# Query, key and value projections of the first linear attention from fp32r high and low parts, on a Trainium2 core

## The reference, cut to what matters

```python
for i in range(8):
    residual = x
    Q  = elu(x @ Wq[i] + bq[i]) + 1      # 16 heads of 64 = 1024 columns
    Kf = elu(x @ Wk[i] + bk[i]) + 1
    V  = x @ Wv[i] + bv[i]
    KV, sumK = sum_s(Kf * V), sum_s(Kf)  # over the 32 tokens of a batch entry
    att = Q * KV / (Q * sumK + 1e-06)
    y = gelu(att @ Wo[i] + bo[i])
    x = layer_norm(y + residual) * ln1_s[i] + ln1_b[i]
    residual = x
    h = gelu(gelu(x @ W1[i] + b1[i]) @ W2[i] + b2[i])
    x = layer_norm(h + residual) * ln2_s[i] + ln2_b[i]
```

## Time and profile before

| | us |
|---|---|
| median of 3 runs (lowest to highest) | 2660.99 (2655.34 to 2661.57) |
| the profiled execution's own time | 2657.94 |
| its span, first to last instruction | 2656.1 |
| attention, first projection (662.0) to last x (1956.3) | 1294.3 |

### The profile page before, as it was taken

The page is one execution under the profiler, slowest core; times in us unless marked ns, Lnnn a source line. Parts: engine busy times, 40 slices in busy tenths (PEclk is TensorE's granted clock), DMA queues, the critical chain, the costliest instruction groups (busy, mean ns, idle before and its releaser), DMA issues. The chain is left out here.

```text
span 2656.1 us, 29174 instructions
## 1 busy us (share of the span) xinstructions
PE 2419.6 (91%) x9257; PEld 1357.0 (51%) x9278; DVE 2144.5 (81%) x2857; ACT 1883.3 (71%) x2673; POOL 791.4 (30%) x466
## 2 busy tenths in 40 slices
PE   7899999998799999999999999999866899757998
PEld 3467776663344444444444444444323677444776
DVE  5787878872899999999999999999857888486454
ACT  6565555654789888998988898888756777435444
POOL 0121121111444444444444444444300000000554
PEclk9999999999899999999999999999986999977999
DMA  2000000002000101001010100100000011310211
GB/s 73 13 21 17 17 20 17 17 1 87 2 0 0 40 1 40 0 0 40 0 40 0 40 0 0 40 0 0 0 12 23 32 40 39 98 41 16 77 65 48
DMA packets 40927, 67.74 MB, mean 26 GB/s; under 512 B 15128, under 2 KB 31832, under 8 KB 39640
## 3 DMA queue, kind: packets, MB, share of 16 engines
q1 hardware_dynamic: 40512, 64.13, 7.4%
q10 hardware_dynamic: 288, 2.10, 0.2%
HBM read 60.91 MB, written 5.31 MB: 25 GB/s over the span
## 5 line engine op out<-in xcount | busy, mean ns | idle before, releaser
L251 PE MATMUL a_ps<-a_x,a_w 128*128 128x512 f32 x1536 | 695.4, 598 | 25.9 <-DVE a_kf L599 13.4
L251 PEld LDWEIGHTS a_ps<-a_x,a_w 128*128 128x128 f32 x1536 | 291.6, 191 | 405.1 <-issue 367.8
L774 POOL TENSOR_TENSOR a_den<-a_qf,a_ksum 128x1024 f32<-128x1024 f32 x128 | 271.0, 2117 | 512.0 <-DVE a_qf L592 475.3
L777 POOL TENSOR_TENSOR a_num<-a_qf,a_kvsum 128x1024 f32<-128x1024 f32 x128 | 294.8, 2303 | 185.5 <-DVE a_kvsum L617 185.5
L2705 ACT ACTIVATE x_sqk<-x_b_k 128x512 f32<-128x512 f32 x256 | 152.9, 597 | 149.1 <-PE x_b_k L2617 142.7
L2781 DVE TENSOR_REDUCE x_rn<-x_sqk 128x8 f32<-128x512 f32 x256 | 174.1, 681 | 91.7 <-ACT x_sqk L2705 87.4
L262 PE MATMUL a_ps<-a_att,a_w 128*128 128x512 f32 x480 | 215.8, 592 | 0.0
L592 DVE SCALAR_TENSOR_TENSOR a_qf<-a_eq,a_qf 128x1024 f32<-128x1024 f32 x128 | 195.2, 1525 | 1.7
L445 ACT ACTIVATE a_den<-a_den,consts 128x1024 f32<-128x1024 f32 x128 | 147.0, 1149 | 55.4 <-POOL a_den L774 55.4
L2598 POOL TENSOR_TENSOR x_kn<-x_craw,x_w 128x256 f32<-128x256 f32 x64 | 47.0, 734 | 464.5 <-DVE x_craw L2770 442.9
L599 DVE SCALAR_TENSOR_TENSOR a_kf<-a_ek,a_ps 128x1024 f32<-128x1024 f32 x128 | 155.4, 1214 | 29.6 <-ACT a_ps L441 24.7
(11 more groups left out here) (423 smaller groups left out, 5189.1 us busy)
## 6 DMA issues: line engine op xcount, KB each, us to landing
a_w<-layers SPq DMA_DIRECT2D x8, 2577.0 KB, 9.7
x_craw<-ctx SPq DMA_DIRECT2D x32, 256.0 KB, 2.7
y_cx<-ctx_t SPq DMA_DIRECT2D x16, 512.0 KB, 3.7
m_wb<-m_scratch SPq DMA_DIRECT2D x16, 512.0 KB, 3.8
n_w<-experts SPq DMA_DIRECT2D x8, 544.0 KB, 5.0
x_w<-xattn_w ACTq DMA_DIRECT2D x1, 1536.0 KB, 9.4
x_all<-x_t SPq DMA_DIRECT2D x4, 256.0 KB, 9.4
...
```

Source lines behind the costliest of these rows:

```text
L251: last = nc.tensor.matmul(bank(tile, j), col(par, part * HK + u * P, P), x[:, t0:t0 + BANK], start=True, stop=True)
L774: nc.gpsimd.tensor_tensor(by_batch(den[:, b, :]), by_batch(qf[:, b, :]), bcast(ksum[:, b, :], S), ALU.mult).then_inc(d_ready, 1)
L777: nc.gpsimd.tensor_tensor(by_batch(num[:, b, :]), by_batch(qf[:, b, :]), bcast(kvsum[:, b, :], S), ALU.mult).then_inc(n_ready, 1)
```

## The change

Every projection is made of three fp32r matmuls in place of one f32 matmul: high weight by high x, high weight by low x, low weight by high x. The high part is a copy into fp32r, the low part the difference. VectorE makes both parts of x at the end of each tail (high x, Hx, from z, and low x, Lx), and TensorE waits for Lx (`x_split`) at the start of a window, now ahead of `out(0)`. GpSimd splits the weights unit by unit (a copy and a subtraction of 128 x 384) in the odd windows 1 to 13, each behind that unit's last projection; SyncE loads each unit's raw weights as the split before ends. The weights of layer 0 are split at the start, and its x by ScalarE (high) and VectorE (low), in four parts. The two gelus of a tail write back into tile_t instead of g, which takes waits for g away; the gelus of W1 write into att, so hid is gone. ScalarE's q part waits for GpSimd behind its exponential and no longer ahead of it. The order is another on every engine; GpSimd's list is written out too.

The diff, without these lists and without what only follows from the rest:

```diff
+UCOLS = 3 * P
+RCOLS = WCOLS + BCOLS - CH * UCOLS
...
+        x_hi, x_lo = (sb(n, [P, TOK], F32R) for n in ("x_hi", "x_lo"))
+        w = sb("w", [P, 2, RCOLS])
+        w_raw = sb("w_raw", [P, UCOLS])
+        w_hi, w_lo = (sb(n, [P, CH, UCOLS], F32R) for n in ("w_hi", "w_lo"))
...
-        hid = sb("hid", [P, FCH, HALF])
-
+
+        first_raw = att[:, 1, 0:3, :].rearrange("p a b -> p (a b)")
...
+            sp.dma_start(first_raw, layers_dram[0][:, 0:CH * UCOLS]).then_inc(first_loaded, 16)
             for par in range(2):
-                sp.dma_start(w[:, par, :], layers_dram[par]).then_inc(w_loaded[par], 16)
+                sp.dma_start(w[:, par, :], layers_dram[par][:, CH * UCOLS:]).then_inc(w_loaded[par], 16)
...
+                for layer in range(LAYERS - 1):
+                    for u in range(CH):
+                        sp.wait_ge(w_split, 8 * layer + u + 8)
+                        sp.dma_start(w_raw[:, :], layers_dram[layer + 1][:, u * UCOLS:(u + 1) * UCOLS]).then_inc(raw_loaded, 16)
+                    if layer + 2 < LAYERS:
+                        wait_ahead(sp, affine, 4 * layer + 4)
+                        sp.wait_ge(x_high, 2 * layer + 2)
+                        sp.dma_start(w[:, layer % 2, :], layers_dram[layer + 2][:, CH * UCOLS:]).then_inc(w_loaded[layer % 2], 16)
...
+                def project(v, half, u, part):
+                    n = 8 * v + u
                     tile, free, ready = ((tile_q, q_parts, q_ready), (tile_k, k_feat, k_ready),
                                          (tile_v, kv_prod, v_ready))[part]
                     wait_past(pe, free, n)
+                    if not half:
+                        pe.wait_ge(w_split, 4 * v + (u + 1))
+                    c = slice(part * P, (part + 1) * P)
                     for j in range(2):
-                        t0 = half * HALF + j * BANK
-                        last = nc.tensor.matmul(bank(tile, j), col(par, part * HK + u * P, P),
-                                                x[:, t0:t0 + BANK], start=True, stop=True)
+                        t = slice(half * HALF + j * BANK, half * HALF + (j + 1) * BANK)
+                        for p, (a, b) in enumerate(((w_hi, x_hi), (w_hi, x_lo), (w_lo, x_hi))):
+                            last = nc.tensor.matmul(bank(tile, j), a[:, u, c], b[:, t], start=(p == 0), stop=(p == 2))
                     last.then_inc(ready, 1)
...
-                    out(0)
                     if not half:
                         pe.wait_ge(w_loaded[par], 4 * v - 8 * par + 16)
-                    wait_ahead(pe, affine, 2 * v - 2)
+                    pe.wait_ge(x_split, v + 1)
+                    out(0)
+                    out(2)
+                    k_of(0)
                     q_of(0)
-                    k_of(0)
-                    out(2)
                     v_of(0)
-                    q_of(1)
                     k_of(1)
                     out(4)
+                    q_of(1)
+                    k_of(2)
                     v_of(1)
-                    k_of(2)
                     out(6)
                     q_of(2)
                     v_of(2)
...
+                    wait_past(act, q_feat, n - 1)
+                    act.wait_ge(q_ready, n + 1)
+                    nc.scalar.activation(eq[:, b, :], tile_q[:, :], ACT.Exp, bias=bias(par, C_BQ + u)).then_inc(q_exp, 1)
+                    wait_past(act, d_ready, n - 1)
                     wait_past(act, n_ready, n - 1)
-                    act.wait_ge(q_ready, n + 1)
-                    nc.scalar.activation(eq[:, b, :], tile_q[:, :], ACT.Exp, bias=bias(par, C_BQ + u))
                     nc.scalar.activation(qf[:, b, :], tile_q[:, :], ACT.Relu, bias=bias(par, C_BQ + u)).then_inc(q_parts, 1)
...
-                    wait_ahead(act, normed, 2 * v)
                     wait_ahead(act, wo_done, v + 1)
-                    nc.scalar.activation(g[:, :], tile_t[:, :], ACT.Gelu_apprx_tanh, bias=bias(par, C_BO)).then_inc(gelu_done, 1)
+                    nc.scalar.activation(tile_t[:, :], tile_t[:, :], ACT.Gelu_apprx_tanh, bias=bias(par, C_BO)).then_inc(gelu_done, 1)
...
+                for p in range(4):
+                    c = slice(p * BANK, (p + 1) * BANK)
+                    nc.scalar.activation(x_hi[:, c], x[:, c], ACT.Copy).then_inc(first_high, 1)
...
+                def high_of(half, scale, shift):
+                    nc.vector.tensor_scalar(x_hi[:, half * HALF:(half + 1) * HALF], z[:, :], scale, shift,
+                                            ALU.mult, ALU.add).then_inc(x_high, 1)
...
+                    def high_x():
+                        if tail:
+                            wait_ahead(dve, normed, 2 * tv + 2)
+                            high_of(th, bias(tp, C_S2), bias(tp, C_B2))
+
+                    def low_x():
+                        if tail:
+                            t = slice(th * HALF, (th + 1) * HALF)
+                            dve.wait_ge(x_high, v)
+                            wait_ahead(dve, affine, 2 * tv + 2)
+                            nc.vector.tensor_tensor(x_lo[:, t], x[:, t], x_hi[:, t], ALU.subtract).then_inc(x_split, 1)
...
+                def numerator(n, b):
                     pool.wait_ge(kv_summed, n + 1)
+                    pool.wait_ge(q_feat, n + 1)
...
+                def split_unit(u, raw, done):
+                    nc.gpsimd.tensor_copy(w_hi[:, u, :], raw).then_inc(w_high, 1)
+                    pool.wait_ge(w_high, done + 1)
+                    nc.gpsimd.tensor_tensor(w_lo[:, u, :], raw, w_hi[:, u, :], ALU.subtract).then_inc(w_split, 1)
...
+                    def split(u):
+                        if half and more:
+                            for ready in (q_ready, k_ready, v_ready):
+                                pool.wait_ge(ready, 8 * v + (u + 1))
+                            pool.wait_ge(raw_loaded, 64 * v + (16 * u - 48))
+                            pool.sem_inc(w_begun, 1)
+                            split_unit(u, w_raw[:, :], 4 * v + (u + 4))
...
+                pool.wait_ge(first_loaded, 16)
+                for u in range(CH):
+                    split_unit(u, first_raw[:, u * UCOLS:(u + 1) * UCOLS], u)
+                all_windows(pool, window, tail_alone)
```

More of the change, by code:

```diff
@@ L231, in all_windows @@
             window(last + 1, 1, 0, True)
-            window(last + 2, 1, 1, True)
+            window(last + 2, 1, 1, True, False)
             tail_alone(last + 2, 1)
@@ L397, in down_part @@
                             pe.wait_ge(hid_gelu, 4 * v + 4 * j + c + 1)
-                            last = nc.tensor.matmul(bank(tile_t, j), col(par, C_W2 + c * D, D), bank(hid[:, c, :], j),
+                            last = nc.tensor.matmul(bank(tile_t, j), col(par, C_W2 + c * D, D), bank(hid(1, c), j),
                                                     start=(c == 0), stop=(c == FCH - 1))
@@ L629, in add_residual @@
                     wait_ahead(dve, affine, z_read)
-                    nc.vector.scalar_tensor_tensor(out=z[:, part], in0=g[:, part], scalar=1.0, in1=resid,
+                    nc.vector.scalar_tensor_tensor(out=z[:, part], in0=tile_t[:, part], scalar=1.0, in1=resid,
                                                    op0=ALU.mult, op1=ALU.add).then_inc(z_added, 1)
@@ L635, in centre, with normalise @@
                     nc.vector.tensor_tensor(z[:, part], z[:, part], tile_t[:, part], ALU.subtract).then_inc(z_centred, 1)
-                def normalise(k, out, scale, shift, part=slice(0, HALF)):
+                def normalise(k, part=slice(0, HALF)):
                     dve.wait_ge(rstd, k + 1)
@@ L640, in normalise, with scale_shift @@
                                                    op0=ALU.mult, op1=ALU.mult).then_inc(normed, 1)
+                def scale_shift(k, out, scale, shift, part=slice(0, HALF)):
                     wait_ahead(dve, normed, k + 1)
@@ L645, in x_of, with window @@
                     return x[:, half * HALF:(half + 1) * HALF]
-                def window(v, par, half, tail):
+                def high_of(half, scale, shift):
+                    nc.vector.tensor_scalar(x_hi[:, half * HALF:(half + 1) * HALF], z[:, :], scale, shift,
+                                            ALU.mult, ALU.add).then_inc(x_high, 1)
+                def window(v, par, half, tail, more=True):
                     tv, tp, th = v - 1, par if half else 1 - par, 1 - half
@@ L765, in _ @@
                     dve.sem_inc(sem_ahead, 1)
+                for p in range(4):
+                    c = slice(p * BANK, (p + 1) * BANK)
+                    dve.wait_ge(first_high, p + 1)
+                    ins = nc.vector.tensor_tensor(x_lo[:, c], x[:, c], x_hi[:, c], ALU.subtract)
+                    if p % 2:
+                        ins.then_inc(x_split, 1)
                 all_windows(dve, window, tail_alone)
@@ L769, in _, with denominator @@
             def _(pool):
-                def unit(n, b):
+                def denominator(n, b):
```

(46 more changed lines are left out.)

250 lines of the change are left out of this document (139 added, 111 removed).

## The result

The change makes the kernel slower: 2858.43 us (median of 4 runs, 2853.05 to 2861.47) against 2661.19, a ratio of 1.0744, 95% interval 1.0720 to 1.0769. The profiled execution took 2861.47, 203.5 more than that of before.

What follows compares the result with a forecast made beforehand. TensorE was fullest (76.48 of 78 us), but the tail's chain over all engines set the window: 88.75 + 2.8 + 1.0 = 92.5 us. 15 windows +216, window 1 -7, start +4 on 2657.94: forecast 2872, range 2650 to 2925.

Steps and rivals of the forecast that it cites:

- the case's own range: Whole kernel, ends of the slower case: windows of 86.0 to 96.3 us, 2774 to 2928 us, upper end taken as 2925.
- The floors: Each engine's work in a window: TensorE 68.6 us with fp32r steps of 0.236, VectorE 75.0, ScalarE 70.1.
- The walk: Chain through the four engines' new lists, from the end of one Lx to the next: 88.75 us for 78.11.
- Both waits: TensorE stands 5.5 us at out0 for Lx; ScalarE's q4 relu, ready at 47.1, waits for den2, ending 53.25.
- The clock: TensorE's gaps at x and ahead of up2 lower its clock: 1.8 and 1.0 us a window.
- The splits: GpSimd, odd windows: a split between num2 and den2, 1.4 us, one ahead of den5, 0.7; 1.0 on the mean.
- The sum: Whole kernel: 15 windows +216, window 1 -7, start +4, so +213 on 2657.94: 2871, given as 2872 us.
- The text's last step: From the profiled execution's 2871 us to the median, 3 us above that execution: given as 2872.
- Only the start of the window hurts: The relus of q3 and q4 do not stand: window 81.4 us, 2704 us in all (2670 to 2760); chance 0.25.
- q4's stand: ScalarE's relu of q4, ready since 47.1, waits for GpSimd's den2, which ends at 53.25.
- Faster: TensorE was the bound and the waits vanish; VectorE's 75.0 us decide: 2616 us (2585 to 2645); chance 0.15.
- its condition: The faster case decides if Fk0 begins within 5.1 us of Lx and den2 ends before q4's exponential.

Runs made afterwards that it cites:

- Run 11: The changed kernel with TensorE's wait for x behind out2, A0 ahead of N0, other lists reordered around N0 and Lx, and Fk4 ahead of Pkv3: 2638.71 us, ratio 0.9918.
- run 4: The changed kernel with GpSimd's copy and subtraction of the weight split left out in the windows, only semaphores counted: 2855.58 us, ratio 1.0742.
- run 2: The changed kernel with A0 ahead of N0 in VectorE's list, no longer behind Fk4: 2772.58 us, ratio 1.0424.
- run 1: The changed kernel with TensorE's wait for the split x moved behind out0 and out2, ahead of k0: 2796.09 us, ratio 1.0516.
- run 9: The changed kernel with the wait for x behind out2, A0 and Fq2 ahead of N0, and three more waits taken out of the lists: 2661.70 us, ratio 1.0006.

## Why the prediction was right

2872 was forecast, 2858.43 came, inside the case's own range and slower as said. By its steps:

- **The floors.** TensorE no longer bounds: the fp32r step is 0.233, for the 0.236 of the earlier trace rows, over 16 steps of TensorE's timeline:

```profile
734.07 0.39 PE L272 MATMUL a_ps<-a_x_lo,a_w_hi 128*128 128x512 f32 x1
...
737.80 0.40 PE L272 MATMUL a_ps<-a_x_hi,a_w_lo 128*128 128x512 f32 x1
```

The 131 ns that the Trainium skill's TensorE: Matmul & The Clock Gate, section Back-to-back issue gap, gives were not seen; the measured step decides. Run 11 has VectorE at 74.06 busy us in a window, for the 75.0.

- **The walk.** From the end of Lx (1004.43) the marks came, forecast in brackets: R0 29.3 (27.25), N0 43.7 (41.85), W1's gelus 57.3 (54.3), W2's 73.9 (71.2), R1 76.4 (73.65), N1 87.3 (84.5), the end of Lx 91.8 (88.75). With the 2.8 that the text charged for the clock beside the walk, 88.75 is 91.55, for an even window of 91.8. Stretch by stretch: R0 to N0 14.45 (14.6), N0 to the gelus 13.6 (12.45), the gelus to W2's 16.6 (16.9), R1 to N1 10.9 (10.85). Both waits stand where the text put them: out0 6.04 us for Lx (5.5), q4's relu 7.40 (6.2), q3's 1.80 (1.85).
- **Two misses that cancel.** From N0 to W1's gelus the walk was 1.15 short: num2 stood 2.56 us (4.47 less 1.91) where the walk let it stand 1.1 for Fq3 and den2 then stand for C4; num and den together ended 0.9 later. From the end of W1's gelus to W2's it was 1.25 long: 10.0 us (1068.33 to 1078.33), walked as 11.25. That the walk ends so close is to that extent luck.
- **The clock.** Behind the wait for x it cost 2.6 in the even windows and 1.1 in the odd ones, 1.85 on the mean of the 14 (1.8). The odd window in TensorE's timeline and in the stages view, where the clock is back at 1.00 3.0 us behind Lx (in the even one the stage 1009 to 1010 is still at 0.50):

```profile
912.10 8.55 PE L282 MATMUL a_ps<-a_att,a_w 128*128 128x512 f32 x16 [5.70 <-DVE a_x_lo L742]
...
920.09 0.80 PE L272 MATMUL a_ps<-a_x_hi,a_w_hi 128*128 128x512 f32 x1
```

```profile
915.00:916.00 1.00, 1.00 (x4) 0.48 (x3) 1.00 (x2) 0.00 (x0) 1.00 (x1) 1.00 0.14 51
```

Why the odd windows lose less was not settled. At up2 the gelus and their load took 6.56 (1061.77 to 1068.33) for 5.60 in the earlier trace rows, so 0.96 (1.0). Fk0 stood 8.80 in the even window, not 5.5, most of it the same 2.6; in the odd ones 5.6 to 7.3.
- **The splits.** They cost an odd window 1.9 us, 1.5 ahead of q4 and 0.4 behind N1, as run 4 shows, so 0.9 on the mean (2.1 and 1.0). The odd window of the stages view is only 0.64 longer than the even one because its shorter time at the lower clock behind x brings R0 1.2 us sooner.
- **The sum.** The text took 78.11 for every window of before; two of them are 2.4 and 2.2 longer and the last three 0.8 (below), and the mean is 78.60. So the 14 windows cost 14 x (92.06 - 78.60) = 188 and not 14 x 14.4 = 202. The other 15 of the 203.5, where the text had 11, lie at the start, in windows 0 and 1 and behind the last: the first projection begins at 668.76 for 662.00, 6.8 where the text had 4. The text's last step slips by 2: 2871 and the 3 of the median are 2874.
- **The rivals.** "Only the start of the window hurts" falls: run 2 changes nothing at the start and gives 86 us, and run 1 leaves 1.0516. (Its sum takes 7.3 for q4's stand, which by the walk's own marks, 47.1 to 53.25, is 6.2; 82.5 in place of 81.4 lies in its range as well.) "Faster" falls for these lists: the two waits that the text held against it are 155 of the 197 us that the change cost. But its condition does not decide. In its even windows run 9 meets it, with Fk0 4.8 us behind Lx and den2 done at 1005.13, ahead of q4's exponential, and is as fast as before; run 11 is faster with Fk0 at 4.8 as well and q4's relu standing 1.55 us for den2. Run 11 has N0 sooner, 34.2 behind Lx for 37.2. ScalarE's timeline, run 9, then run 11:

```profile
1008.29 1.11 ACT L455 ACTIVATE a_eq<-a_ps,a_w 128x1024 f32<-128x1024 f32 x1 [3.28 <-PE a_ps L272]
```

```profile
1007.32 1.12 ACT L458 ACTIVATE a_qf<-a_ps,a_w 128x1024 f32<-128x1024 f32 x1 [1.55 <-POOL a_den L856]
```

- **A row misread.** The earlier trace rows shows VectorE idle 2.94 us ahead of Fk0, and the text compared its 5.5 with that. That row is from a window in which the loop closes; it and one other (2.71 us) have such a wait. In the windows that begin at 806.80, 884.92 and 963.03, as in the others with a tail, Fk0 does not wait. No term of the sum hung on it.

Shown by runs is what taking out the two waits gives, 62 and 86 us and 155 together, and what fp32r gives. The clock's part is read from rows alone: no run had the gaps without it.
